# Two attention layers and a mixture of experts over a graph: node runs found by ranks, a blank row, and carries from the ring

## The reference

```python
x = x + gat1(layernorm(x), edge_index)      # 4 heads x 64 features, W 256x256
x = x + experts(layernorm(x), edge_index)   # 2nd attention: 4 heads x 4 features, then top 2 of 4 MLPs

# gat1, per edge (row, col), and per head
e   = leaky_relu(h_l[row] + h_r[col], 0.2)
m   = segment_max(e, row);  ex = exp(e - m[row])
out = segment_sum(ex / segment_sum(ex, row)[row] * h[col], row)
# second attention: the same over dst, with 6250 self loops appended; its 16 numbers per node
# are layer-normed into 4 expert scores; top 2; out = sum_g w_g * (gelu(x W1 + b1) W2 + b2)
```

## Time and profile before

| | |
|---|---|
| median of 3 runs | 4602.96 us (4595.94 to 4609.97) |
| profiled execution | 4600.72 us, span 4599.0 us |
| granted clock of TensorE, mean | 0.658 of 2.4 GHz |
| PE / DVE / ACT / POOL busy | 1994.8 / 1905.6 / 590.9 / 1901.0 us |
| gathers of the first attention, POOL L1744 | 792, 804.7 us busy |
| adds, PE L1808 | 1584 matmuls, 578.6 us |
| one-hots of the counts, DVE L343 | 228, 156.6 us busy; idle before them 298.3 |
| matmuls of the counts, PE L383 | 1824 recorded, 190.9 us |
| gathers of node sums, POOL L878 | 98, 124.1 us |

### The profile page before, as it was taken

One profiled execution on the slowest core, in us unless ns is written; L12 is line 12 of the kernel. 1 busy time (PEld: TensorE's weight loads), 2 busy tenths in 40 slices (PEclk: granted clock), 3 DMA queues, 4 the chain that ended last, 5 costly groups with the idle time before them and its releaser, 6 DMA issues. The chain is left out here.

```text
span 4599.0 us, 28729 instructions
## 1 busy us (share of the span) xinstructions
PE 1994.8 (43%) x8658; PEld 1511.8 (33%) x8658; DVE 1905.6 (41%) x3756; ACT 590.9 (13%) x1135; POOL 1901.0 (41%) x1909
## 2 busy tenths in 40 slices
PE   5236033444434453555541244435464443446720
PEld 3125022322223342434430133324343332334510
DVE  7789555444644643536510121121222112222657
ACT  4100011111111111111310001101010100101000
POOL 0015735445445544441767434444333344432032
PEclk9555566666666665656565667768787776778855
DMA  3111333443443433334521011111101011110415
GB/s 123 17 37 26 92 132 114 139 141 113 143 137 110 151 133 107 132 121 155 137 66 16 12 27 21 20 28 27 27 18 33 14 20 28 28 27 18 151 50 185
DMA packets 196305, 353.72 MB, mean 77 GB/s; under 512 B 55253, under 2 KB 160651, under 8 KB 192792
## 3 DMA queue, kind: packets, MB, share of 16 engines
q0 software_dynamic: 73264, 122.12, 12.2%
q1 hardware_dynamic: 73823, 181.16, 10.8%
q10 hardware_dynamic: 49132, 49.53, 3.2%
HBM read 181.17 MB, written 171.59 MB: 77 GB/s over the span
## 5 line engine op out<-in xcount | busy, mean ns | idle before, releaser
L533 POOL DMA_INDIRECT at_ring<-table,e_col x872 | 828.9, 951 | 1064.9 <-DMA at_sums<-at_ring 803.2
L1744 POOL DMA_INDIRECT at_ring<-table,at_idx x792 | 804.7, 1016 | 253.2 <-issue 233.9
L1808 PE MATMUL at_psS<-at_ring,at_hot 128*128 128x260 f32 x1584 | 578.6, 528 | 633.5 <-issue 371.5
L1808 PEld LDWEIGHTS at_psS<-at_ring,at_hot 128*128 128x128 f32 x1584 | 381.9, 260 | 825.0 <-issue 538.5
L769 PE MATMUL pick_rows<-pick_table,late_space 128*128 128x272 bf16 x1368 | 212.2, 314 | 703.6 <-issue 359.8
L1305 PE MATMUL ffn_psH<-xnT,late_space 128*128 x896 | 385.0, 591 | 196.6 <-ACT late_space L1340 188.5
L1368 DVE TENSOR_TENSOR late_space<-ffn_psY,ffn_b 128x256 f32<-128x256 f32 x196 | 82.5, 424 | 915.9 <-PE ffn_psY L1316 492.2
L1316 PE MATMUL ffn_psY<-late_space 128*128 128x256 f32 x1568 | 381.3, 405 | 162.6 <-issue 91.4
L769 PEld LDWEIGHTS pick_rows<-pick_table,late_space 128*128 128x128 bf16 x1368 | 143.5, 109 | 760.6 <-issue 364.7
L1316 PEld LDWEIGHTS ffn_psY<-late_space 128*128 128x128 f32 x1568 | 316.8, 204 | 224.8 <-issue 102.8
L1305 PEld LDWEIGHTS ffn_psH<-xnT,late_space 128*128 128x128 f32 x896 | 276.6, 312 | 297.4 <-ACT late_space L1340 196.3
(11 more groups left out here) (349 smaller groups left out, 2253.6 us busy)
## 6 DMA issues: line engine op xcount, KB each, us to landing
at_sums<-at_ring SPq DMA_DIRECT2D x24, 4356.0 KB, 12.1
products<-late_space ACTq DMA_DIRECT2D x28, 896.0 KB
late_space<-products SPq DMA_DIRECT2D x16, 896.0 KB, 11.7
at_ring<-table,e_col POOLq DMA_INDIRECT x872
at_ring<-table,at_idx POOLq DMA_INDIRECT x792
at_sums<-at_ring SPq DMA_DIRECT2D x16, 768.0 KB, 3.2
late_space<-products ACTq DMA_DIRECT2D x12, 896.0 KB, 11.2
table<-np_rows SPq DMA_DIRECT2D x7, 910.0 KB, 4.2
```

Of the source, the lines that this page charges most:

```text
L533: g.indirect_dma_start(self.ring[z][:, k, 0:TW], None, self.table, bass.IndirectOffsetOnAxis(ap=self.runs.col[:, u * U + k:u * U + k + 1], ...
L1744: g.indirect_dma_start(self.ring[z][:, k, 0:self.TW], None, self.table, bass.IndirectOffsetOnAxis(ap=self.idx[:, z, k:k + 1], axis=0)).the ...
L1808: last = pe.matmul(self.psS[at % 2][:, k - lo, 0:TW], self.hot[:, b, k, :], rows[:, b * self.SUB + k, 0:TW], start=True, stop=True)
```

## The change

1. **Ranks in place of counts.** `Ranks` takes the place of `Counts`. `past` (one DVE pass, 128 x 49 x 128, from iota in PSUM) marks for each partition of the sorted list which of each tile's 128 node codes are past its first row. `differences` forms each code's difference to the code of the partition before, in two bf16 parts. It needs the codes shifted by a partition, `prior`, a DMA of its own. For each of 49 node tiles, `rows` multiplies `past[t]` with the two parts in two column halves (the matmul adds the differences up to the last partition that the node is not past), two bf16 matmuls of 400 or 512 columns for each; `below` compares the half in PSUM with the node code and counts what is below it by the accumulator of the same operation (98 of them for a list). Two PSUM halves take turns. The first list's 98 halves are unrolled; the second has 1 tile ahead and 16 a round, in shares of 4+4, 4+4, 0+0.
2. **A blank row.** `sums` has one more row, written once (0, and -BIG for the maxima); nodes without edges get its index as their end, and POOL's clearing of `acc` goes.
3. **Carries from the ring.** In the last round SP copies the last row of each group from the ring to `carry` before the store; the load behind the stores goes.
4. **Collect** is split. `begin_vector` comes first in the middle block, `spread.clear` and `mid.prepare` come last, and 17 small operations become six, three of them ahead of the wait for the sums.
5. **Second attention:** the factor is in PSUM, and the weights are copied to the rows before the scans.

```diff
@@ class Ranks (in place of Counts)
+    def past(self, v, code):
...
+        q.step(v.tensor_tensor(t.past[:, :, :], self.iota.unsqueeze(1).to_broadcast([P, T, P]),
+                               t.first_row[:, :].unsqueeze(2).to_broadcast([P, T, P]), ALU.is_gt))
+    def differences(self, v, code, prior, one, two):
...
+        for part, mask in enumerate((((1 << bits) - 1) << (COL_BITS + LANE_BITS), (P - 1) << COL_BITS)):
+            q.step(v.tensor_scalar(one, code, mask, None, ALU.bitwise_and))
+            q.step(v.tensor_scalar(two, prior, mask, None, ALU.bitwise_and))
+            q.wait()
+            q.step(v.tensor_tensor(t.parts[:, part, 0:J], one, two, ALU.subtract))
+            q.wait()
+        v.sem_inc(self.s_parts, 1)
+    def rows(self, pe, at, first, i):
+        t, H = self.t, self.H
+        past = t.past[:, bass.ds(at + i, 1), :].rearrange("p o q -> p (o q)")
+        for half in range(2):
+            pe.wait_ge(self.s_used, first * 2 + (2 * i + half + 1))
+            pe.matmul(self.ps[half], past, t.parts[:, 0, half * H:(half + 1) * H], start=True, stop=False)
+            pe.matmul(self.ps[half], past, t.parts[:, 1, half * H:(half + 1) * H], start=False, stop=True)\
+                .then_inc(self.s_rows, 1)
+    def below(self, v, at, first, i):
+        t, H = self.t, self.H
+        for half in range(2):
+            v.wait_ge(self.s_rows, first * 2 + (2 * i + half + 1))
+            v.tensor_scalar(t.less[:, half, 0:H], self.ps[half], t.node[:, bass.ds(at + i, 1)], 0.0, ALU.is_lt, ALU.add,
+                            accum_out=t.n[:, bass.ds(at + i, 1), half]).then_inc(self.s_used, 1)
+    def end_rows(self, pe):
...
+        for i in range(T):
+            last = pe.matmul(self.ps_many[:, i:i + 1], t.past[:, i, :], t.one[:, :], start=True, stop=True)
@@ class Runs
+    def load_prior(self, a):
+        a.wait_ge(self.s_sorted, self.sorted)
+        a.dma_start(self.prior[1:P, :].bitcast(F32), self.code[0:P - 1, :]).then_inc(self.s_prior, 16)
@@ class Attend
-        self.factor = sb("factor", [P, 2, HEADS, U])
+        self.factor = ctx.enter_context(nc.psum_tensor(f"{tag}_factor", [P, 2, HEADS, U], F32))
...
+        q.step(v.tensor_copy(rows[:, :, D:D + HEADS], weight.rearrange("p h u -> p u h")))
@@ Collect.fix
-        g.memset(self.acc[:, :, 0:D + HEADS], 0.0).then_inc(self.s_empty, 1)
-        g.memset(self.acc[:, :, D + HEADS:W], -BIG).then_inc(self.s_empty, 1)
@@ Collect.vector
-        spans = [(h * F, (h + 1) * F, h) for h in range(HEADS)] + [(D + h, D + h + 1, h) for h in range(HEADS)]
-        for a, b, h in spans:
-            q.step(v.tensor_scalar(self.tail[:, a:b], self.tail[:, a:b], self.scale[:, 1, h:h + 1], None, ALU.mult))
-        q.wait()
-        for a, b, h in spans:
-            q.step(v.scalar_tensor_tensor(out=self.part[:, a:b], in0=self.ps_sum[:, a:b], scalar=self.scale[:, 0, h:h + 1],
-                                          in1=self.tail[:, a:b], op0=ALU.mult, op1=ALU.add))
...
+        q.step(v.tensor_tensor(by_head(self.part), by_head(self.ps_sum), spread(0), ALU.mult))
@@ ChainAttend.sync, in the last round and behind it
+            if not more:
+                sp.dma_start(self.carry[z * WIDE:(z + 1) * WIDE, :],
+                             self.ring[z][LIVE - 1:LIVE, :, :]).then_inc(self.s_carry, 16)
...
-        sp.dma_start(self.carry[0:CHAINS, :], self.sums[last:last + CHAINS, :]).then_inc(self.s_carry, 16)
@@ shares of the second search
-            ahead, per_round = 8, 40
-            shares = [range(0, 7), range(7, 14), range(14, 20), range(20, 27), range(27, 33), range(33, per_round)]
+            ahead, per_round = 1, 16
+            shares = [range(0, 4), range(4, 8), range(8, 12), range(12, per_round), range(0), range(0)]
@@ rest rounds, scalar
+                    found2.load_prior(a)
@@ middle block, vector
+                        col.begin_vector(v)
+                        mid.pad(v)
+                        col.vector(v)
                         spread.clear(v)
-                        mid.pad(v)
                         mid.prepare(v)
-                        col.vector(v)
                         mid.vector(v)
```

272 lines of the change are left out of this document (149 added, 123 removed).

## The result

| | before | after |
|---|---|---|
| median on one chip, 4 runs of each | 4599.45 us | 4637.77 us (4632.71 to 4643.01) |
| ratio, 95% interval | | 1.0076 [1.0058, 1.0093] |
| span of the profiled execution | 4599.0 us | 4631.0 us |
| PE / DVE / ACT / POOL busy | 1994.8 / 1905.6 / 590.9 / 1901.0 us | 1920.3 / 1848.7 / 589.7 / 1864.8 us |

A forecast was written before the change was run, and what follows sets the result against it. No engine was busy for half the span, so each stage's chain was taken as the bound; 6 + 4 + 8 + 0 - 3 - 13 - 2 + 5 = +5 on 4600.72 gave 4606 us, range 4570 to 4640.

The forecast's parts named there:

- rival 2: Searches beside gather bursts: two-half PE-to-DVE hand-over turns late, five searching units lose 20 to 50 us; 4636, chance 0.2.
- First search, +6: Counting of the first edge list: longer prelude, 98 halves at 0.83 us and a 9.3 us tail end at 421.5, against 415.45.
- the prelude grows: Start of the first search: `past` 6.9 us, small operations about 1, `differences` 4.1, `lanes` gone; first half in PSUM about 331.
- Second search, +4: First searching unit of the rest rounds: DVE work starts at 1582 instead of 1563, mostly absorbed by the burst; +1 to +19.
- I take 1568 for its landing: Second search: ACT's 512 KB load of `prior`, issued about 1557.5 beside a 4.4 MB store, lands at 1568.
- Units, +8 at the end: Last round of the first attention: 16, 16 and 0 halves replace 14, 13 and 13 groups; +8 us (+5 to +14).
- Rival 1: First-attention units beside bursts fall back to a turning round's pace, 66.7 us; seven units give -32, 4574; chance 0.2.
- Rival 3: First search runs at the lower bound, 0.70 us a half: -13, 4593, chance 0.15; at 1.0, 4623, chance 0.1.
- Carry, -3: Seam after the last store: dropping the carry's load saves 3.5 us, a small copy costs 0.4; -3 us.
- Middle, -13: Middle block: earlier start -4.6, L905 without memset -8.5, fewer small operations -1.8, loads beside gathers +2; -5 to -15.
- Second attention, +5: Sixteen units: added weight copy and factor read from PSUM cost 0.4 to 0.6 us each, about 10 on the chain; 0 to +15.
- rival 4: Middle block: L905 was long for another reason than the memset, the block gains 5 and not 13; 4614, chance 0.05.

The follow-up runs named there:

- e1: The change with the first list's load of `prior` on SP split into 112 and 15 rows: 4641.13 us, 1.0031 of the kernel before.
- e2: The change with the second list's load of `prior` on ACT split into 112 and 15 rows: 4646.09 us, 1.0036 of the kernel before.
- e3: The change with both loads of `prior` split into 112 and 15 rows: 4631.81 us over 12 runs, 0.9998 of the kernel before.
- e8: The change with both loads split and the second attention as before (factor in SBUF, no copy), on a quick chip: 3137.34 us, 0.998 of the kernel before.
- e4: The change with POOL's two memsets of `acc` put back, blank row kept: 4666.32 us, 1.0078 of the kernel before.

## Why the prediction was right or wrong

**The total: in the range, by two errors that the range happened to hold.** The sum said 4606 and no difference; the measured 4638 stands where rival 2 had put its 4636, but the change was not slow by rival 2's account. Two terms were 40 us too low, mostly for the load of `prior`, to which the sum gave nothing in the first search and too little in the second, and that the time fell inside the range is luck. One of the text's own signs of being wrong appeared, a unit of 96.7 us beside a burst, over the 84, and the scatters start at 438.26, outside 416 to 428.

**What bounds the kernel: right where it was used.** The first search shifts the first attention nearly one for one: its end moved by 21.9 us (the cast of L366, 415.45 to 437.37 with its successor's end), the first store by 24.9. The other 3 us were not followed.

**First search, +6: a missing term and a low one.** The step that failed is "the prelude grows": it priced `past`, the casts and the differences, and never the DMA of `prior`, though the account of the change names it as a DMA of its own. The prelude's own work was right to 0.1 us; the load cost 12.66 (e1: 11.5 us sooner without it). The rule to see it stands in the Trainium skill (DMA: Bandwidth & Descriptors, "Why a DMA increments its semaphore by 16 and not by 1"): a transfer is spread over the largest number of DMA engines up to 16 that divides its slowest dimension, which for 127 rows is one. The trace agrees, at 26 GB/s against 219 and more with the load in 112 and 15 rows. The halves took 0.91 us and not 0.83, +8; but that number averages some 0.66 away from the gathers and in their first 15 us, and 2.6 from 352 to 384. "PE's clock stays at 0.50" was wrong too: the granted clock was 0.93 from 384 to 432, and there DVE is the busier of the two (43.46 of 48 us against PE's 38.07), so the comparison with its accumulator sets the pace and not PE's 0.70. The tail took 4.5 us and not 9.3, because 49 one-column matmuls cost 1.4 us in all. 12.7 + 8.3 - 4.8 is the 16 us between 421.5 and 437.4.

**The accumulator** shows as a record of its own of 0.09 us behind each comparison of 0.64 us. The Trainium skill's rule of two instructions (VectorE: DVE Perf Modes, "Two Vector instructions with no wait between them") holds; but the comparisons run at 0.66 us a half, so it was not what cost.

**Second search, +4: mis-sized by 21.** The step "I take 1568 for its landing" gave the load 10.5 us; it took 40. In the change this wait accounts for the whole 25.4: the one-hots start 27.9 us behind their 1609.8, and the halves then run behind the burst and are not late. The split gives the load 11 us and still takes only 8 us off the unit (e2), because the halves then fall late in the burst and idle for 25 us (e3): by that, some 17 of the 25.4 would have been lost with the load as early as the step had it, too. The step had bounds of +1 to +19, and +25.4 lies beyond them.

**Rival 2: the mechanism right, the place half.** It was priced at five searching units. In the later units of the change nothing is late: each share of eight halves starts either 6.3 us behind the start of a burst or behind its last gather, and its last seven halves idle 0.8 to 1.5 us in all; the six units came out at -6.2. It bites where halves fall later in a burst: in the first search, which the rival did not look at, and, once the load is split, in the first unit of the second. That the four buffers are what kept the old searches from it is likely (11 groups with 0.5 us of idle time) but not shown: in the first search the old gathers also came only every 1.75 us, and neither was changed alone.

**Units, +8 at the end: right** (+7.1). **Rival 1** (back to 66.7 us) did not happen: the units beside bursts take 69 to 75 us. **Rival 3** (a first search at 0.70 us a half) did not either: it came to 0.66 away from the burst, but to 0.91 over all.

**Carry, -3: wrong in size.** The load behind the stores went, and 0.7 us was gained. What the block's end waits for is then the last store, it seems: 14.84 us from its issue to the next block's first DMA after, against 15.53 before.

**Middle, -13: right in the main** (-12.4 to the first gather of the node sums, -15.6 to the first of the second attention), in its parts too high for the memset (5.1 net, not 8.5) and too low for the rest, since the earlier put lands more slowly.

**Second attention, +5: wrong in sign** (-3.6). **Last block, -2: right** (-2.2). The copy costs 0.42 us a unit as predicted. Where the gain comes from is open: on this chip the gathers of that stage did not change. That operands in PSUM leave POOL's descriptors alone stood beside rival 4 as a rule, with 4600 for the sum. The gathers of the first attention bear it out here, beside a search that reads PSUM in place of SBUF: 1016 ns before and 984 after over all 792. The difference lies where a search runs: 1.45 and 0.95 us in the first search, 998 and 960 ns in the rest rounds, but 978 and 972 in the turning rounds, which have none. In the rest rounds that makes 9 us of POOL in seven bursts, and the six further units gained 6.2 us. On quick chips the same effect decides the second attention (e8).

**Open.** Why a result of PE reaches DVE some 4 us late beside gathers on some chips and not on others is not explained by any run: the same kernels, the same clock levels. That the lateness grows during a burst (1.46 to 4.96 us) and ends with it looks like work that piles up; what piles up the traces do not show. The deeper ring and the later gathers were not tried on such a chip.

## What to carry to other kernels

Price every DMA that a change adds, by its shape as much as by its bytes: a tile shifted by one partition has 127 rows, and splitting two such loads into 112 and 15 took 45 us off this kernel at 3139. A hand-over with two buffers costs where it falls late in a burst of gathers, and little at its start or behind it, so look at when each share runs before pricing it; a loss may also hide behind another, as in the second search, and show only when the first is mended. Repeat a verdict of under one per cent on a second chip before it is trusted: this change is 0.8% slower on one, and between level and 0.4% faster on another, where the kernel before itself falls into two groups 20 us apart.

## What the runs showed of the hardware that was not expected

- One kernel takes 4599 to 4628 us in two sets of runs and 3142 to 3143 on two other chips. The first attention's units take some 69 us beside a burst on the first kind and some 40 on the second, with gathers of about 1 us on both.
- A DMA of 127 rows moves 26 GB/s, and the issue of the next load behind it on SP (L1585) took 8.39 us, where it takes 0.44 with the 127 rows split (e1).
- Small DVE and POOL operations meet at full cost: 0.23 us becomes 8.70 beside a memset of 10.74, repeated in e4 to the hundredth. POOL's gathers took 57 ns more each in e8, whose second attention has its factor in SBUF, and 1.45 in place of 0.95 us beside the old first search.
- The hand-over between PE and DVE was not late in the first 15 us of a burst of gathers, then up to 4.96 us late, and on time again some 6 us behind its last gather, on one kind of chip only.
- The best version is e3, the change with both loads split: 0.9814 [0.9774, 0.9854] of the kernel before on a quick chip (0.984 by the medians), 45 us below the change, and level with the kernel before (0.9998 [0.9981, 1.0015]) on the chip of e1 to e4.
